# Moving the row terms of a quantised product behind the layer norm, and reordering the opening loads, in an attention-and-FFN kernel on one core

## The reference

```python
def _L0_xattn_ref(x1, x2, x1_scale, x1_zp, x2_scale, x2_zp):
    q1 = fake_quant(x1, x1_scale, x1_zp)
    q2 = fake_quant(x2, x2_scale, x2_zp)
    return jnp.matmul(q1, q2)                       # (2,1024,2048) x (2,2048,2048)

def _L0_ffn_ref(x, gate, kernel, bias, lora_A, lora_B, lora_A_shared, lora_B_shared):
    base_out = jnp.matmul(x, kernel) + bias
    x_flat = x.reshape(b, -1, x.shape[-1])          # 8 groups of 256 tokens
    A_eff = jnp.einsum('bn,nri->bri', gate, lora_A)
    B_eff = jnp.einsum('bn,nor->bor', gate, lora_B)
    ...                                             # delta = B_eff (A_eff x) + B_shared (A_shared x)
    return base_out + delta

x = x + _L0_xattn_ref(_layernorm(x), ctx_4096, ...)
x = x + _L0_ffn_ref(_layernorm(x), ...)
```

## Time and profile before

| | |
|---|---|
| median of 3 runs | 1063.55 us |
| the profiled execution | 1063.74 us, of which the span 1061.7 us |
| TensorE busy | 1003.1 us (94%) |
| VectorE busy | 532.3 us (50%) |
| ScalarE busy | 311.5 us (29%) |
| GpSimd busy | 163.4 us (15%) |
| mean granted TensorE clock | 0.989 |

### The profile page before, as it was taken

How to read it: one execution, slowest core, us unless ns; L and a number is a source line. 1 busy time by engine, 2 the same in 40 slices (tenths; PEclk the granted TensorE clock), 3 DMA queues, 4 the chain that set the end, 5 groups by cost and what they waited for, 6 DMA issues and landing times.

```text
span 1061.7 us, 12294 instructions
## 1 busy us (share of the span) xinstructions
PE 1003.1 (94%) x4791; PEld 472.9 (45%) x4791; DVE 532.3 (50%) x764; ACT 311.5 (29%) x266; POOL 163.4 (15%) x199
## 2 busy tenths in 40 slices
PE   2778999799999999999999999999999999999996
PEld 1345444355544444444444444445544444444442
DVE  6754677879655455463423555987632023014010
ACT  4666731322032132232223743532121021003000
POOL 3101100101102211311510000020104004004110
PEclk9989999899999999999999999999999999999998
DMA  8869682767735446338599844456935025004010
GB/s 365 255 192 368 260 346 96 184 139 183 201 127 195 168 149 212 138 112 251 204 299 262 336 179 159 80 166 147 222 110 169 20 80 187 20 30 158 10 42 27
DMA packets 124392, 181.70 MB, mean 171 GB/s; under 512 B 96064, under 2 KB 96064, under 8 KB 111808
## 3 DMA queue, kind: packets, MB, share of 16 engines
q1 hardware_dynamic: 109600, 118.25, 37.3%
q0 software_dynamic: 13600, 58.73, 15.3%
q10 hardware_dynamic: 1152, 4.19, 1.0%
HBM read 128.72 MB, written 29.36 MB: 149 GB/s over the span
## 4 chain that ended last, share of the span: by engine, by line
PE 68%; DVE 11%; DMA 10%; issue 4%; ACT 3%; POOL 1%; SPq 1%; DVEq 0%; POOLq 0%; ACTq 0%
PE psum L1154 16%; PE psum L1156 16%; PE psum L1155 16%; PE psum L987 15%; DMA stage<-in_w 2%; DMA x<-in_x 2%; PE psum L1177 2%; DMA lhs<-in_lora_b 1%; DVE ring L1396 1%; DMA xn<-in_x 1%; DVE stats L1421 1%; DVE hl L1441 1%; DVE stats L1308 1%; DMA bias_sb<-in_bias 1%; DMA lhs<-ap_st 1%
## 5 line engine op out<-in xcount | busy, mean ns | idle before, releaser
L1154 PE MATMUL psum<-ring,lhs 128*128 128x512 f16 x1024 | 388.8, 380 | 9.4 <-DMA lhs<-hl 7.4
L1155 PE MATMUL psum<-ring,lhs 128*128 128x512 f16 x1024 | 388.8, 380 | 0.0
L1156 PE MATMUL psum<-ring,lhs 128*128 128x512 f16 x1024 | 388.8, 380 | 0.0
L987 PE MATMUL psum<-ring,lhs 128*128 128x512 bf16 x1024 | 235.2, 386 | 9.0 <-DMA lhs<-ap_st 7.1
L987 PEld LDWEIGHTS psum<-ring,lhs 128*128 128x128 bf16 x1024 | 101.4, 99 | 134.8 <-issue 15.4
L1154 PEld LDWEIGHTS psum<-ring,lhs 128*128 128x128 f16 x1024 | 100.3, 98 | 132.3 <-issue 10.1
L1156 PEld LDWEIGHTS psum<-ring,lhs 128*128 128x128 f16 x1024 | 100.4, 98 | 121.3 <-issue 0.8
L1155 PEld LDWEIGHTS psum<-ring,lhs 128*128 128x128 f16 x1024 | 100.3, 98 | 119.9 <-issue 0.8
L1448 DVE SCALAR_TENSOR_TENSOR x<-psum,sc,x 128x512 f32<-128x512 f32 (+1 forms) x64 | 45.3, 746 | 182.2 <-PE psum L1166 181.4
L748 ACT ACTIVATE ring<-stage,sc 128x2048 f16<-128x2048 f32 x32 | 63.7, 2002 | 202.6 <-PE psum L1156 159.4
L617 POOL TENSOR_TENSOR x<-x,bias_sb 128x512 f32<-128x512 f32 (+1 forms) x64 | 87.7, 1396 | 173.5 <-DVE xn L1431 98.2
(11 more groups left out here) (158 smaller groups left out, 644.9 us busy)
## 6 DMA issues: line engine op xcount, KB each, us to landing
stage<-in_w SPq DMA_DIRECT2D x38, 1024.0 KB, 6.0
stage<-in_ctx_in SPq DMA_DIRECT2D x30, 1024.0 KB, 7.9
out<-x POOLq DMA_DIRECT2D x64, 256.0 KB, 3.5
x<-in_x POOLq DMA_DIRECT2D x8, 1024.0 KB, 11.9
xn<-in_x POOLq DMA_DIRECT2D x8, 1024.0 KB, 7.3
x<-in_x POOLq DMA_DIRECT2D x4, 2048.0 KB, 15.9
lhs<-in_lora_a POOLq DMA_DIRECT2D x4, 1024.0 KB, 6.9
lhs<-in_lora_b SPq DMA_DIRECT2D x4, 1024.0 KB, 13.3
```

The costliest lines, as they stand in the source:

```text
L987: last = pe.matmul(psum[:, t, :], lhs_q[:, k, t * P:(t + 1) * P], ring_q[:, g, j % 2, u, :], start=(k == 0), stop=False)
L1154: pe.matmul(psum[:, t, :], hi, ring[:, g, 0, u, :], start=(kk == 0), stop=False)
L1155: pe.matmul(psum[:, t, :], hi, ring[:, g, 1, u, :], start=False, stop=False)
L1156: last = pe.matmul(psum[:, t, :], lo, ring[:, g, 0, u, :], start=False, stop=False)
```

## The change

The row term is no longer added before the eviction. ScalarE adds it once per tile over all 2048 columns, in the layer-norm stage, after the norm of that tile has been read; since it is one number for a token's whole row, the norm takes it off anyway. `evict1` no longer waits for it (in batch 1 it waits for the residual's load), and `add_bias` waits for `with_row` in place of `normed2`. On GpSimd the loads of x tiles 4 to 7 stand together, and the first two loads of the LoRA A factor come right after. On SP the four turns stand ahead of the loads of context groups 0 and 1 of block 1, the loads of the LoRA B factor ahead of the last context groups, and the loads of block 2 wait for `be_full` 8. On VectorE `round1(4)` and `round1(5)` come earlier, the copies of B_eff are taken out of `peak_b` (`copy_b`), and `w_group` 0 and 1 stand around `low2(1)`. On TensorE the first pair starts when tile 0 is turned. The number of matmuls is the same, the column term stays a matmul a tile.

```diff
@@ SP @@
             load_ctx(0, 0, [0, 1])
-            load_ctx(0, 1, [0, 1])
             for t in range(PT, TILES):
                 turn_q(t)
+            load_ctx(0, 1, [0, 1])
...
             load_lora_b(0)
+            load_lora_b(1)
             load_ctx(0, 1, [2])
-            load_lora_b(1)
-            load_ctx(0, 1, [3])
             load_lora_b(2)
             load_lora_b(3)
+            load_ctx(0, 1, [3])
+            sp.wait_ge(be_full, 8)
             load_ctx(0, 2, [0, 1])
...
                         turn_y(b, 0)
-                        turn_y(b, 1)
+                        turn_high(b, 1)
+                    if g == 2 and isinstance(j, int) and j == 0:
+                        turn_low(b, 1)
@@ GpSimd @@
-            load_x([4, 5])
+            load_x(range(4, TILES))
             root_pair(1)
-            load_x([6, 7])
...
+            load_lora_a(0)
+            load_lora_a(1)
             root_pair(2)
-            load_lora_a(0)
             root_pair(3)
-            load_lora_a(1)
...
-                        pool.wait_ge(normed2, b * TILES + t + 1)
+                        pool.wait_ge(with_row, b * TILES + t + 1)
@@ ScalarE @@
+                def row_term(t):
+                    act.wait_ge(rows_ready, b + 1)
+                    act.activation(x2[:, t, :], x2[:, t, :], ACT.Identity, bias=RC[:, t:t + 1]).then_inc(with_row, 1)
...
-                    for t in range(TILES):
-                        row_term(t, 0, 1)
                     for c in range(NBLK):
                         for k in range(c * KC, (c + 1) * KC):
                             a_eff_out(k)
-                        ctx_block(b, 1, [c])
+                        if c < 2:
+                            ctx_block(b, 1, [c])
+                    ctx_block(b, 1, [2])
                     for c in range(NBLK):
+                        if c == NBLK - 1:
+                            ctx_block(b, 1, [3])
                         b_eff_out(c)
-                        if c:
-                            row_term(c - 1, 1, NBLK)
                     column(1)
-                    for t in range(NBLK - 1, TILES):
-                        row_term(t, 1, NBLK)
...
                     split_hi(b, t)
                     if t + 1 < TILES:
                         root(b, 1, t + 1)
+                    row_term(t)
...
                 split_hi(b, 1)
+                w_groups(b, 0, [2, 3])
                 root(b, 1, 2)
-                w_groups(b, 0, [2, 3])
+                row_term(0)
+                row_term(1)
@@ TensorE @@
+                    tile_in(0)
+                    bank_free(k, 0)
+                    pe.wait_ge(converted, grp_w(b, 0, 0) + 1)
+                    base_group(0, 0)
+                    high_in(1)
+                    bank_free(k, 1)
+                    high_group(1, 0)
+                    pe.wait_ge(converted, grp_w(b, 0, 1) + 1)
+                    base_group(0, 1)
+                    low_in(1)
+                    low_group(1, 0)
+                    base_group(1, 1)
+                    for g in range(2, NG):
@@ VectorE @@
-                dve.wait_ge(with_row, (2 + j) * TILES + t + 1 if b else min(j, 1) * TILES + t + 1)
+                if b:
+                    dve.wait_ge(res_in[j], 16)
...
             round1(2)
+            round1(3)
             stats1(5, range(2))
-            round1(3)
             turn_out(2)
             stats1(5, range(2, NBLK))
+            variance([4, 5])
             head_group(2)
             turn_out(3)
-            variance([4, 5])
+            scale_rows([4, 5], 3)
             head_group(3)
-            stats1(6)
-            scale_rows([4, 5], 3)
+            stats1(6, range(2))
+            round1(4)
+            stats1(6, range(2, NBLK))
+            round1(5)
             stats1(7)
             variance([6, 7])
-            round1(4)
             scale_rows([6, 7], 4)
-            round1(5)
...
                 evict1(b, j, 3)
-                early_stats2(b, 2)
-                late_stats2(b, 2)
+                w_group(b, 0, 0)
                 low2(b, 1)
+                w_group(b, 0, 1)
                 evict1(b, j, 4)
                 evict1(b, j, 5)
-                w_group(b, 0, 0)
-                w_group(b, 0, 1)
                 evict1(b, j, 6)
                 evict1(b, j, 7)
                 w_group(b, 0, 2)
+                stats2(b, 2)
                 w_group(b, 0, 3)
```

More of the change, by code:

```diff
@@ L637, in _ @@
                     largest(2, MX_B, PW_B)
-                    store_a(b)
+                    store_a(b, range(GPB))
                     largest(3, MX_W, PW_W)
@@ L1146, in last_bases, with high_group, low_group @@
                         base_group(t, g)
+            def high_group(t, g):
+                for u in range(GU):
+                    kk = g * GU + u
+                    hi = lhs[:, 0, kk, t * P:(t + 1) * P]
+                    pe.matmul(psum[:, t, :], hi, ring[:, g, 0, u, :], start=(kk == 0), stop=False)
+                    pe.matmul(psum[:, t, :], hi, ring[:, g, 1, u, :], start=False, stop=False)
+            def low_group(t, g):
+                for u in range(GU):
+                    lo = lhs[:, 1, g * GU + u, t * P:(t + 1) * P]
+                    pe.matmul(psum[:, t, :], lo, ring[:, g, 0, u, :], start=False, stop=False)
             def base_group(t, g):
```

54 lines of the change are left out of this document (25 added, 29 removed).

## The result

| | before | changed |
|---|---|---|
| time, median (lowest to highest, 4 runs each), us | 1063.98 (1063.34 to 1066.58) | 1054.04 (1053.24 to 1055.98) |
| ratio, 95% interval | | 0.9905, 0.9883 to 0.9926 |
| profiled execution, us | 1063.74 | 1053.89 |
| its span, us | 1061.7 | 1051.6 |
| TensorE busy, us | 1003.1 | 998.4 |

Faster by 9.9 us, where 17.8 were forecast; 1054.0 lies just outside the range of 1040 to 1053. In the first 186 us, 13.3 of the 14.4 us forecast for them arrived; behind them part of it was given back.

The account below looks back on a forecast made before the run. TensorE, busy 1003.1 of 1061.7 us, bounds the kernel, so gains lie only in its waits and lower clock. 8.5 + 4.6 + 1.3 + 2.3 + 1.1 = 17.8 off 1063.74 gave 1046 us, range 1040 to 1053.

Parts of the forecast that it names:

- opening: Before the LoRA stage: waits for tile 4's turn and the cold clock go, a column-term wait comes; 8.5 us, bounds 3 and 10.3.
- LoRA factors: LoRA stage: TensorE's two waits for LoRA B loads, 1.45 and 3.18 us, both go; 4.6 us, bounds 0 and 4.6.
- column term of block 1: LoRA stage: TensorE's 1.26 us wait goes as row terms leave ScalarE's list; gain 1.3 us, bounds -1.3 and 1.3.
- second product's start, batch 0: Layer-norm stage: TensorE starts its pair at once, 7.9 us earlier, but keeps only 2.3 us; bounds 0 and 4.
- batch 1: Second batch's layer-norm stage: a 1.24 us wait goes, the fourth weight group ends earlier; gain 1.1 us, bounds -1.5 and 1.2.
- The rival with a shared turn: Opening: a turn still shares its time with a load, so turn 7 or 4 lands late; 1048 to 1052 us, 15 in 100.
- That chain moves by its start alone: Layer-norm stage, batch 0: VectorE, ScalarE and turns go tile by tile in the same order, starting 2.3 to 3 us earlier.
- some 5 us in sum: Layer-norm stage, batch 0: TensorE's expected waits after starting the pair at once, before delta of tile 2.
- The row terms: Layer-norm stage, batch 0: eight on ScalarE, about 2.0 us each, all hidden; if not, the 2.3 us term is lost first.

## Why the prediction was wrong: a chain that does not move by its start alone

| step | forecast | measured | how it reads |
|---|---|---|---|
| opening | 8.5 | 9.4 | A_eff 76.27 to 66.83 |
| LoRA factors | 4.6 | 3.8 | block 1 109.46 to 96.25 is 13.2, less 9.4 |
| column term of block 1 | 1.3 | 0.1 | T 13.34, less 13.2 |
| second product's start, batch 0 | 2.3 | -1.8 | T to D +0.41, slow clock 1.35 |
| between | 0 | -0.8 | weight groups of later blocks |
| batch 1 | 1.1 | -0.7 | T to D +0.72 |
| sum | 17.8 | 10.1 | |

**The opening** was right in its mechanism and nearly in its size: no wait for tile 4, the clock up, turns of 4.4 to 4.8 us. The loads ahead of turn 4 were through by 39, as worked out; no byte moved from 40 to 41.7. One wait I hadn't seen: TensorE stands 1.46 us in the run of 48 for VectorE's PSUM copy (L1367). It cost nothing, by luck: in the kernel before that run began at the lower clock (0.50 from 36 to 38 us) and took 12.04 us, now the clock is up and the 48 take 10.4 beside the wait. I had carried the 12.04 over. The column term waits 1.26 instead of 1.8. The rival with a shared turn fails in this kernel, and the run with a load beside a turn shows it would have cost little.

**The LoRA factors**: one wait of 0.96 stays of 4.6. It ends at 89.11, halfway through B_eff, so it is for the third load, which was issued at 77.7 and took 11.4 us; I had timed only the fourth.

**The column term of block 1**: the step said "the row terms go", and the wait went. What was missed is what is late next on VectorE: the last copy of B_eff behind a context group, and behind that the group itself, which lands at 95.2. The wait only moved to a place ten microseconds earlier. I had put the group's landing at 25 us into the LoRA stage, 92; it was 28.

**The second product's start** is the step that failed, and the sentence is "That chain moves by its start alone". Two things are wrong with it. First the start: the fourth weight load goes out behind the low turn of tile 1, whose issue took 5.31 us beside the weight load ahead of it (3.06 in the kernel before), so the load went out at 192.46; `norm2(2)` is 1.1 us earlier against T, not 2.3 to 3. Second the chain: I followed norm, rounding, turn, and left out the LoRA B rows between tiles 3 and 4, where VectorE stands for a load that SyncE issues behind the turn of tile 3. That link runs over turn, load and conversion, and it took 1.4 us longer than before with the same order (0.54 in the turn's issue, 2.69 for 2.15; the rest from the last of the four transfers to the conversion, 4.2 for 3.4). It swallowed what the start had won. With the link taken out, T to D falls by 2.5 us in the new order and by 2.5 to 3.1 in the old one. In the one trace of the kernel before with the same edit T to D stays, and there TensorE's own time, with its wait of over 6 us at the head, is as long as the chain; the gain of that kernel's time is not explained by it. The profile of before had told this much: a wait of 0.24 at the end of a chain says that the chain and TensorE finish together. TensorE's early start alone was worth 0.24; the other 2 us had to come from every link of the chain, and I had followed it only to the first turns.

The waits that I expected in the stage ("some 5 us in sum") came to 8.0 (0.99, 2.08, 1.00, 1.15, 2.82). I did not ask what waits do to the clock, though the earlier trace rows had shown it: 1.35 us in the profiled execution and 1.67 in the second trace of this kernel.

**The row terms** are hidden, as worked out, at 1.94 to 1.99 us each (3.88 for two).

**Batch 1** fails by the same first half: a turn that took 7.9 us to land beside the weight load. Its second half matters less there, waits of 1.57 and 0.30. In the second trace the loss of 0.7 is 0.0; the gain of 1.1 is in neither. Left open: why the loads of the old order land later behind the new opening. The two weight loads of the old order took 5.1 us in the median in both traces with the old opening, and 5.7, 5.9 and 5.4 in the three with the new one; no more data moved beside them (3.3 MB in the 12 us behind T with the old opening, 3.1 to 3.2 with the new). Open too: what makes VectorE's weight groups late in the later blocks. TensorE's waits for them there are 1.6 us in the kernel before and 2.6 and 3.3 in the two traces of the changed one, and the stretch from D to T of batch 1 lay between 410.1 and 415.6 us over all kernels.

## What to carry to other kernels

A wait near zero at the end of a long chain means that two chains end together: before giving a gain to one, follow the other link by link, over each queue and each load that an engine stands for, and ask what a link hangs on besides the one ahead of it. When a chain is the bound, look for loads that stand on a queue behind work they don't need; moving two such loads (0.9831 for 0.9905) gave more than the whole reordering of the stage had (0.9905 for 0.9919, not to be told apart).
